# Gate and up products as three float32r products of split operands, and a ring of three query and key buffers

## The reference

```python
h = _layernorm(x) * (1 + ca) + sa
Q, K, V = ...                                  # 16 heads of 16
scores = Q @ K.T / 4 + slopes * (k - q)        # causal, then softmax
x = x + ga * ((softmax(scores) @ V) @ o_w.T + o_b)
h = _layernorm(x) * (1 + cb) + sb
hq = fp4_quant_dequant(h)                      # blocks of 16: grid value times the block's scale
gate = hq @ fp4_quant_dequant(w_gate).T        # w_gate, w_up: 704 x 256
y = hq @ fp4_quant_dequant(w_up).T
z = fp4_quant_dequant(silu(gate) * y)
x = x + gb * (z @ fp4_quant_dequant(w_down).T) # w_down: 256 x 704
```

## Time and profile before

| | |
|---|---|
| median of 3 runs | 3683.75 us (3681.61 to 3691.07) |
| the profiled execution, its own time | 3689.2 us |
| its span, first to last instruction | 3687.4 us |
| mean granted TensorE clock | 0.979 of full speed |
| PE, DVE, ACT, POOL busy | 94%, 81%, 52%, 35% of the span |

### The profile page before, as it was taken

The page is one execution under the profiler, slowest core; times in us unless marked ns, Lnnn a source line. Parts: engine busy times, 40 slices in busy tenths (PEclk is TensorE's granted clock), DMA queues, the critical chain, the costliest instruction groups (busy, mean ns, idle before and its releaser), DMA issues.

```text
span 3687.4 us, 56900 instructions
## 1 busy us (share of the span) xinstructions
PE 3475.3 (94%) x20920; PEld 1926.6 (52%) x20920; DVE 2993.7 (81%) x5836; ACT 1924.8 (52%) x3631; POOL 1272.5 (35%) x919
## 2 busy tenths in 40 slices
PE   6889999999999999999999999999999999999987
PEld 2335555555555555555555555555555555555555
DVE  9987978788787888878788787888878788786855
ACT  3455555555555555555555555555555555554541
POOL 5213424243342423324243332523324243342233
PEclk7899999999999999999999999999999999999998
DMA  7242423314333332423314333342423314333010
GB/s 128 41 88 43 70 50 59 66 32 74 53 56 59 50 67 43 70 50 59 66 32 74 53 58 57 50 71 38 71 50 62 64 34 71 53 52 52 23 28 12
DMA packets 160938, 205.34 MB, mean 56 GB/s; under 512 B 44740, under 2 KB 100628, under 8 KB 160660
## 3 DMA queue, kind: packets, MB, share of 16 engines
q1 hardware_dynamic: 160660, 201.69, 32.4%
HBM read 63.65 MB, written 17.89 MB: 22 GB/s over the span
## 4 chain that ended last, share of the span: by engine, by line
PE 69%; DVE 17%; ACT 5%; SPq 4%; DMA 3%; issue 2%; POOL 1%; ACTq 0%; POOLq 0%; DVEq 0%
PE banks L758 13%; PE banks L782 11%; PE banks L739 9%; PE banks L879 8%; PE banks L886 8%; PE banks L902 6%; PE banks L809 5%; DVE banks L1208 4%; DVE top L1206 4%; ACT arena L971 3%; PE banks L860 3%; SPq L619 2%; DMA sums<-oT 2%; PE banks L742 1%; PE banks L895 1%
## 5 line engine op out<-in xcount | busy, mean ns | idle before, releaser
L971 ACT ACTIVATE arena<-banks 128x512 f32<-128x512 f32 (+1 forms) x2432 | 1235.0, 585 | 941.9 <-PE banks L758 508.5
L1208 DVE CUSTOM_DVE_ANT_0 banks<-banks,mask 128x640 f32<-128x640 f32 (+3 forms) x1024 | 1031.7, 1045 | 155.4 <-PE banks L782 147.5
L739 PE MATMUL banks<-qa,ka 105*128 105x512 bf16 (+3 forms) x3072 | 784.5, 329 | 52.4 <-ACT arena L971 27.2
L782 PE MATMUL banks<-ka,qa 102*128 102x512 bf16 (+3 forms) x3072 | 751.5, 333 | 55.7 <-DVE top L1208 21.9
L758 PE MATMUL banks<-arena,va 128*17 128x512 f32 (+3 forms) x6144 | 585.6, 500 | 12.1 <-ACT arena L971 4.1
L1105 POOL TENSOR_TENSOR hid<-hid,tm 128x704 f32<-128x704 f32 x128 | 214.9, 1679 | 911.6 <-DVE hid L1182 911.6
L782 PEld LDWEIGHTS banks<-ka,qa 102*128 102x128 bf16 x3072 | 259.1, 99 | 421.9 <-DVE top L1208 103.5
L739 PEld LDWEIGHTS banks<-qa,ka 105*128 105x128 bf16 x3072 | 273.3, 97 | 392.5 <-ACT arena L971 126.9
L1206 DVE TENSOR_REDUCE top<-banks 128x2 f32<-128x768 f32 (+3 forms) x384 | 386.4, 1041 | 102.7 <-PE banks L787 101.2
L902 PE MATMUL banks<-wdT,hqT 128*128 128x256 f32 x1536 | 367.3, 390 | 4.1 <-ACT hqT L1014 3.8
L879 PE MATMUL banks<-wguT,xqT 128*128 128x352 f32 x1024 | 332.4, 467 | 3.2 <-ACT arena L971 2.5
(11 more groups left out here) (152 smaller groups left out, 4603.4 us busy)
## 6 DMA issues: line engine op xcount, KB each, us to landing
qa<-parts SPq DMA_DIRECT2D x384, 128.0 KB, 4.6
ka<-parts SPq DMA_DIRECT2D x384, 128.0 KB, 6.3
xa<-in_x SPq DMA_DIRECT2D x16, 1024.0 KB, 10.1
xr<-in_x SPq DMA_DIRECT2D x64, 256.0 KB, 2.7
out_x<-xr SPq DMA_DIRECT2D x64, 256.0 KB, 3.4
rsumT<-rsum_dram SPq DMA_DIRECT2D x63, 256.0 KB
onT<-oT SPq DMA_DIRECT2D x252, 64.0 KB, 4.1
ffn_rows<-rows_dram SPq DMA_DIRECT2D x16, 256.0 KB, 3.2
```

The lines of the kernel that those rows point to most:

```text
L739: mm = pe.matmul(ps[:, m * w:(m + 1) * w], ka[g][0:KT, h, kt * P:(kt + 1) * P], qa[g][0:KT, h, q0:q0 + w], start=heads < G and m == 0, sto ...
L782: mm = pe.matmul(ps[:, at:at + z - a], qa[g][0:KS, h0 + m, qt * P:(qt + 1) * P], ka[g][0:KS, h0 + m, a:z], start=qt > 0 and m % paired == ...
L971: nc.scalar.activation(probs[:, s % P_SLOTS, j * heads:(j + 1) * heads, 0:w], ps[:, 0:heads * w].rearrange("p (h q) -> p h q", h=heads), A ...
L1208: nc.vector.tensor_tensor_reduce(out=ps, in0=ps, in1=mask[:, S - w:S], scale=1.0, scalar=MASKED, op0=ALU.add, op1=ALU.max, accum_out=tops) ...
```

## The change

- **Products.** `xqT` and `wguT` each become two float32r tensors, high and low. The high part is ScalarE's copy of the PSUM bank into a float32r tensor; the low part is a new DVE instruction (XL for the rows, WL for the weights) that subtracts the high part from the same bank. A product is high x high, high x low, low x high, summed in PSUM: three float32r matmuls in place of one float32 matmul. GA waits for XL through `low_done`, and the bank of XT and of WT is held until DVE has read it.
- **Ring.** There are three buffers of queries and keys in place of four, used in turn: group n (counted over all batches) has buffer n mod 3, and its MOVE waits for the last T of group n - 3, in place of n - 4. In the plan it also stands behind TOP of group n - 2, and its due time is later by a quarter of a batch.
- **Slope rows.** A buffer no longer belongs to one group, so the six slope rows have to be renewed each time. QROW writes them into borrowed memory (`slope_stage`), SROW copies them to DRAM (two DMAs per group, once), and each MOVE of queries begins with a seventh DMA that brings them in. KROW fills three buffers.
- **Plan.** `SHIFT` has other numbers, the planned costs of GA and UP are 0.95 and 1.9 in place of 1.2 and 2.4, and the U events have later due times.

The diff, its added and removed lines only, cut to the core:

```diff
+LANDED = {"q": 16 * (len(Q_PARTS) + 1), "k": 16 * len(K_PARTS)}
+SETS = 3
+def earlier(b, g, n):
+    return divmod(b * NG + g - n, NG)
...
-    SHIFT = {"ACT CO": 42.0, "ACT GA": -43.0, "ACT HT": -8.0, "ACT KROW": 78.0, "ACT LX": 22.0, "ACT T": -74.0,
...
+    SHIFT = {"ACT CO": 32.0, "ACT GA": -46.0, "ACT HT": -5.0, "ACT KROW": 62.0, "ACT LX": 2.0, "ACT T": -104.0,
...
-            p.add("SP", ("MOVE", b, u, g), 3.9, at + (g + 1) * L / NG, ("POOL", ("SPL", b, u)),
-                  ("PE", ("T", b - 1, g, NS - 1, jobs_of(NS - 1) - 1)), ("SP", ("TOP", b - 1, g + 1)) if g + 1 < NG else None, lag=6.0)
+            p.add("SP", ("MOVE", b, u, g), 4.5 if UNITS[u][0] == "q" else 3.9, at + (g + 2) * L / NG, ("POOL", ("SPL", b, u)),
+                  ("PE", ("T", *earlier(b, g, SETS), NS - 1, jobs_of(NS - 1) - 1)), ("SP", ("TOP", *earlier(b, g, SETS - 1))),
+                  ("SP", ("SROW", 0, g)) if b == 0 else None, lag=6.0)
...
-            p.add("DVE", ("QROW", 0, g), 2.8, -30.0 + 20.0 * g, ("DVE", ("QROW", 0, g - 1)))
-            p.add("ACT", ("KROW", 0, g), 3.6, -30.0 + 20.0 * g, ("ACT", ("KROW", 0, g - 1)))
+            p.add("DVE", ("QROW", 0, g), 4.8, -60.0 + 5.0 * g, ("DVE", ("QROW", 0, g - 1)), ("SP", ("SROW", 0, g - 1)))
+            p.add("SP", ("SROW", 0, g), 1.3, -60.0 + 5.0 * g, ("DVE", ("QROW", 0, g)), lag=4.0)
+            if g < SETS:
...
-               ring="A", on="ACT", takes_cost=0.59)
+               ring="A", on="ACT", takes_cost=0.59, holder=("DVE", ("XL", b, r)))
+            p.add("DVE", ("XL", b, r), 0.69, due + 9, ("ACT", ("XT", b, r)))
-                    pe(("GA", b, t, k), 1.2, due + 10 + k, ("ACT", ("XT", b, r)), ("PE", ("HT", *tile(2 * r - 1), 1)),
+                    pe(("GA", b, t, k), 0.95, due + 10 + k, ("DVE", ("XL", b, r)), ("DVE", ("WL", 0, GU // 2)), ("PE", ("HT", *tile(2 * r - 1), 1)),
-                pe(("UP", b, t), 2.4, late + 2, ("PE", ("GA", b, t, 1)), ("PE", ("UP", *tile(t - 1))), ring="D", on="DVE",
+                pe(("UP", b, t), 1.9, late + 2, ("PE", ("GA", b, t, 1)), ("PE", ("UP", *tile(t - 1))), ring="D", on="DVE",
...
+LOW = {e: n for n, e in enumerate((e for e in PLAN.order["DVE"] if e[0] in ("WL", "XL")), 1)}
+WEIGHTS_LOW = max(LOW["WL", 0, n] for n in range(GU // 2 + 1))
...
-        qa = [sb(f"qa{g}", [P, G, S], BF16) for g in range(NG)]
-        ka = [sb(f"ka{g}", [P, G, S], BF16) for g in range(NG)]
+        qa = [sb(f"qa{n}", [P, G, S], BF16) for n in range(SETS)]
+        ka = [sb(f"ka{n}", [P, G, S], BF16) for n in range(SETS)]
-        xqT = [sb(f"xqT{n}", [P, C, 2 * P]) for n in range(2)]
+        xqT = [[sb(f"xqT{part}{n}", [P, C, 2 * P], F32R) for part in "hl"] for n in range(2)]
-        wguT = sb("wguT", [P, C, 2 * FF])
+        wguT = [sb(f"wguT{part}", [P, C, 2 * FF], F32R) for part in "hl"]
...
+        slope_stage = [t.bitcast(BF16) for t in (rsumT[:, :], onT[:, C - 1, :])]
...
-                    dst, order = (qa[g], Q_PARTS) if name == "q" else (ka[g], K_PARTS)
+                    qs, ks = group_set(b, g)
+                    dst, order = (qs, Q_PARTS) if name == "q" else (ks, K_PARTS)
-                    if b:
-                        sp.wait_ge(a_full, in_a["T", b - 1, g, NS - 1, jobs_of(NS - 1) - 1])
+                    if b * NG + g >= SETS:
+                        sp.wait_ge(a_full, in_a["T", *earlier(b, g, SETS), NS - 1, jobs_of(NS - 1) - 1])
+                    if name == "q":
+                        if b == 0:
+                            sp.wait_ge(slopes_out, 32 * g + 32)
+                        sp.dma_start(dst[SPLIT:KS, :, :].rearrange("p h q -> p (h q)"), slope_dram[g]).then_inc(part_in[u, g], 16)
-                    sp.dma_start(qa[g][KS:KT, :, :], topT[g % 2][:, :]).then_inc(top_in[g], 16)
+                    sp.dma_start(group_set(b, g)[0][KS:KT, :, :], topT[g % 2][:, :]).then_inc(top_in[g], 16)
+                elif kind == "SROW":
+                    g = e[2]
+                    sp.wait_ge(static_rows, G * g + G)
+                    for n in range(2):
+                        sp.dma_start(slope_dram[g][:, 2 * n * S:(2 * n + 2) * S], slope_stage[n][SPLIT:KS, :]).then_inc(slopes_out, 16)
...
+                low = [LOW[o] for o in PLAN.before[e] if o in LOW]
+                if low:
+                    pe.wait_ge(low_done, max(low))
...
-                        src = xqT[(t // 2) % 2][:, :, (t % 2) * P:(t % 2 + 1) * P]
+                        high, low = (part[:, :, (t % 2) * P:(t % 2 + 1) * P] for part in xqT[(t // 2) % 2])
+                        terms = [(x[:, c, :], w[:, c, :]) for c in range(C) for x, w in ((high, wguT[0]), (high, wguT[1]), (low, wguT[0]))]
-                            for c in range(C):
-                                mm = pe.matmul(ps[:, 0:FH], src[:, c, :], wguT[:, c, e[3] * FH:(e[3] + 1) * FH],
-                                               start=(c == 0), stop=(c == C - 1))
+                            pe.wait_ge(low_done, max(LOW["XL", b, t // 2], WEIGHTS_LOW))
+                            for n, (x, w) in enumerate(terms):
+                                mm = pe.matmul(ps[:, 0:FH], x, w[:, e[3] * FH:(e[3] + 1) * FH],
+                                               start=(n == 0), stop=(n == len(terms) - 1))
-                                for c in range(C):
-                                    mm = pe.matmul(ps[:, k * BANK:k * BANK + FH], src[:, c, :],
-                                                   wguT[:, c, FF + k * FH:FF + (k + 1) * FH],
-                                                   start=(c == 0), stop=(c == C - 1))
+                                for n, (x, w) in enumerate(terms):
+                                    mm = pe.matmul(ps[:, k * BANK:k * BANK + FH], x, w[:, FF + k * FH:FF + (k + 1) * FH],
+                                                   start=(n == 0), stop=(n == len(terms) - 1))
...
-                        nc.scalar.copy(xqT[e[2] % 2][:, :, :], ps[:, :].rearrange("p (c n) -> p c n", c=C)).then_inc(a_free, 1)
+                        nc.scalar.copy(xqT[e[2] % 2][0][:, :, :], ps[:, :].rearrange("p (c n) -> p c n", c=C)).then_inc(a_free, 1)
...
+                        if g:
+                            dve.wait_ge(slopes_out, 32 * g)
-                            nc.vector.tensor_scalar(qa[g][SPLIT:KS, i, :], ones[SPLIT:KS, :],
+                            nc.vector.tensor_scalar(slope_stage[i // 2][SPLIT:KS, i % 2 * S:(i % 2 + 1) * S], ones[SPLIT:KS, :],
...
+                        r = e[2]
+                        high, low = xqT[r % 2]
+                        dve.wait_ge(a_free, in_a["XT", b, r])
+                        nc.vector.tensor_tensor(low[:, :, :], bank(("XT", b, r)).rearrange("p (c n) -> p c n", c=C),
+                                                high[:, :, :].bitcast(F32), ALU.subtract).then_inc(low_done, 1)
```

More of the change, by code:

```diff
@@ L12 @@
 BF16 = mybir.dt.bfloat16
+F32R = mybir.dt.float32r
 I32 = mybir.dt.int32
@@ L229, in plan, with pe @@
     L = 240.0
-    def pe(event, cost, due, *after, ring, on, takes_cost, then=(), lock=None, banks=1):
-        p.add("PE", event, cost, due, *after, lag=0.22, ring=ring, lock=lock, banks=banks)
+    def pe(event, cost, due, *after, ring, on, takes_cost, then=(), lock=None, banks=1, holder=None):
+        p.add("PE", event, cost, due, *after, lag=0.22, ring=ring, lock=lock, banks=banks, holder=holder)
         p.add(on, event, takes_cost, due, ("PE", event), *then, takes=ring)
@@ L277, in maxima @@
                    *([("SP", ("MOVE", b, u, g)) for u in (2 * (g // 2), 2 * (g // 2) + 1)]
-                     + [("DVE", ("QROW", b, g)), ("ACT", ("KROW", b, g))] if j == 0 else ()),
+                     + [("ACT", ("KROW", b, g))] if j == 0 else ()),
                    ring="D", on="DVE", takes_cost=(0.14 if w <= BANK else 0.29) + 1.042e-3 * w * heads, banks=-(-heads * tile_pitch(heads, w) // BANK),
@@ L326, in normalise @@
         p.add("SP", ("RDW", b, g, *half), 0.7, due, ("DVE", ("RD", b, g, *half)), ("SP", ("RBC", *old)), lag=6.0)
-        p.add("SP", ("RBC", b, g, *half), 0.7, due, ("SP", ("RDW", b, g, *half)), ("POOL", ("MUL", b, g // 2 - 1) if g >= 2 else ("MUL", b - 1, C - 1)), lag=7.0)
+        p.add("SP", ("RBC", b, g, *half), 0.7, due, ("SP", ("RDW", b, g, *half)), ("SP", ("SROW", 0, NG - 1)), ("POOL", ("MUL", b, g // 2 - 1) if g >= 2 else ("MUL", b - 1, C - 1)), lag=7.0)
         if g % 2:
@@ L542, in bank, with group_set @@
             return banks[:, first * BANK:(first + number) * BANK]
+        def group_set(b, g):
+            n = (b * NG + g) % SETS
+            return qa[n], ka[n]
         in_a, in_d, in_q = NUMBER["A"], NUMBER["D"], NUMBER["Q"]
@@ L990, in run @@
                         act.wait_ge(a_full, full)
-                        nc.scalar.copy(wguT[:, :, 2 * n * P:(2 * n + tiles) * P],
+                        nc.scalar.copy(wguT[0][:, :, 2 * n * P:(2 * n + tiles) * P],
```

(2 more changed lines are left out.)

49 lines of the change are left out of this document (33 added, 16 removed), and 13 rows, old and new, of the table SHIFT.

## The result

The changed kernel takes 3574.58 us in the median (3573.87 to 3578.04) against 3682.95 us (3681.61 to 3691.07) for the kernel before, measured side by side. The ratio is 0.9703, with a 95% interval of 0.9686 to 0.972. The forecast was 3574.

What follows compares the result with a forecast made beforehand. PE was taken as the bound, with DVE near enough to disturb it. Fifteen batches at 7.5 us won give 112.5; with 7 lost at the start and 4 won at the end, 109.5 us, so 3574 median, range 3530 to 3640.

Steps and rivals of the forecast that it cites:

- start: Before batch 1: QROW's waiting rounds and WL's six subtractions, less a quantising pass moved back, lose 7 us, 0 to 15.
- PE's busy time in a batch: Gate and up products: 3.60 us a tile in place of 4.73, so 9.0 us less for a batch of eight tiles.
- last batch and its end: Batch 15's feed-forward runs alone: 6 us won on its chain pieces, 2 us given back to XL, 4 us won taken.
- I take the lower bound, 0.150: Gate and up products: a float32r matmul of 352 columns streams one column per clock, as bfloat16, and costs 0.150 us.
- neither bound: Price of a 352-column float32r matmul: between 0.150 us at one clock per column and 0.296 us at two.
- rival of two clocks per column: Gate and up products: float32r streams at 0.296 us a matmul, 7.10 us a tile, total about 3985 us; chance 6%.
- My estimate by that rule: Gate and up products with every weight load added: a tile goes from 6.4 to 6.1 us, little won.
- rival of the loads as the pace: Gate and up products: weight loads of 0.190 us set the pace, 4.56 us a tile, total 3680 us; chance 4%.
- I take the middle, 1.5 us: PE's idle time per batch: grows 1.5 us, between none and 3.0, as DVE's free time falls from 39.7 to 29.
- the rival took 4.8: GA waits for DVE's late XL, about 1.2 us for each of four pairs, 4.8 a batch, total 3646 us; chance 17%.
- 40 us of slack on SP: Ring and slope DMA: MOVE needs 15 us of a group's 55, so both were priced at nothing.
- moves too late: SP reaches MOVE over 40 us late, S starts late, each microsecond per group costs 64; 3766 us at 3 us; chance 2%.

Runs made afterwards that it cites:

- one-product kernel: Changed kernel, order and XLs kept, but gate and up each one float32 product of the unsplit operand: 3687.66 us, ratio 0.9999 to the kernel before.
- bfloat16 run: Changed kernel with the high and low tensors in bfloat16 in place of float32r, same 24 matmuls a tile: 3546.36 us in one run.
- old table: Changed kernel with only SHIFT put back to the numbers of the kernel before, new U due times kept: 3719.12 us, ratio 1.0091 to the kernel before.
- ring alone: Changed kernel with single float32 products, no XL or WL: 3689.40 us with new SHIFT and U due times, 3755.69 us with those of the kernel before.
- Table b: Changed kernel with another SHIFT, found by small random steps that did not lengthen the planned time: 3561.11 us, ratio 0.9661 to the kernel before.

## Why the prediction came out right, step by step

Its mechanism holds: cheaper products shorten PE's busy time, PE stays the bound, and ring, slope rows and XL are hidden, XL all but half a microsecond a batch. The range is earned by that. That the total was hit to 1 us is luck, since the start came out 14.5 us better than entered and the end 14.5 us worse. The terms:

| term | predicted | measured |
|---|---|---|
| one float32r matmul, 352 columns | 0.150 us | 0.159 us |
| PE's busy time in a batch | -9.0 us | -7.8 us |
| PE's idle time in a batch | +1.5 us | -0.1 us |
| a batch | 7.5 us won | 7.85 us won |
| start | 7 us lost | 7.5 us won |
| last batch and its end | 7.5 + 4 us won | 3.0 us lost |

**The products.** The step "I take the lower bound, 0.150" was 9 ns short. 24 x 0.159 is 3.82 us a tile, 0.91 less than before and not 1.13, 7.3 us a batch; the one-product kernel, its order held fixed, has 7.1 us more of PE's busy time a batch and a period 7.0 longer. The rest of the 7.8 us came with the order and the clock. The bfloat16 run shows that the working was right for that type and that float32r carries 10 ns more. The spacing crossed neither bound and stayed under 0.16. The weight loads, 188 ns each, don't set the pace: matmuls stand 0.159 and 0.13 us apart. A float32r matmul takes one pass of its columns, and the rival of two clocks per column is out. The Trainium skill's "TensorE: Matmul & The Clock Gate" ("The mechanism") says that a load overlaps matmuls in flight only when it goes to another row group; these rows contradict that, as the earlier trace rows do. The same section of the Trainium skill also lets a load into the array's spare weight buffer go ahead, which these rows would fit. My estimate by that rule had a slip, 24 x 0.257 is 6.2 us and not 6.1. So had the rival of the loads as the pace: it comes to some 3689 us and not 3680 (20 won, 22.5 lost to idle time, 3 at the two ends).

**PE's idle time.** The step "I take the middle, 1.5 us" entered a cost that is not there. Idle time stayed at 7.9 us, though DVE's free time fell by 14 us where I had worked out 11: DVE is busy 186.5 us a batch, 6.0 more than before, and XL is only 2.7 of them. That free time is no measure: with DVE busy 188.7 PE is idle 13.7 us under the old table, with 186.5 it is 7.9 under the new one, and the ring alone with its two tables has 10.9 and 8.0. The order of the lists matters more. The error of the spacing (192 x 9 ns, 1.7 us a batch) and this one (1.6) cancelled, which is luck too.

**XL.** Its 0.69 us (686 ns in the median) and the cover for GA's wait are confirmed: 1.5 us of waiting in all, and without XL thirteen of the periods are 0.5 us shorter, where the rival took 4.8.

**Ring and slope rows at nothing.** Right for the kernel as it is: 0.9994 to 1.0012 for the ring alone, nothing from the slope DMAs. But the reason given, 40 us of slack on SP, was too weak. With that slack and the old table the ring costs 68 us. The rival "moves too late" priced this as S standing for MOVE. No run shows PE stand there for long; the loss comes with the order that the planner builds under the ring's rules.

**Start.** QROW's four rounds ran as described, and their waits for the copies were short. Timeline of DVE:

```profile
37.62 3.47 DVE L1291 TENSOR_SCALAR rsumT<-arena,xb 6x1024 bf16<-6x1024 f32 x2 [4.60 <-DMA slope_dram<-onT]
...
47.62 2.56 DVE L1291 TENSOR_SCALAR rsumT<-arena,xb 6x1024 bf16<-6x1024 f32 x2 [2.10 <-DMA slope_dram<-onT]
...
71.71 5.80 DVE L1251 TENSOR_REDUCE top<-banks 128x4 f32<-128x512 f32 x6
```

6.70 us of waiting, and the first eviction of S at 71.71, 3.2 us earlier than before, not later. The products give 4.2 us up to batch 1 (one product against after), the order 3.3.

**End.** The products pay there as worked out, 12.4 us against 11.5. But the order lost 15 where I had entered nothing. In the chain of after, a gate product early in the feed-forward of batch 15 and the next one are 29.8 us apart:

```profile
3467.49 3.86 PE banks L925 x12
3471.35 2.60 PE banks L932 x12
...
3497.28 3.18 PE banks L925 x12
```

The corresponding pieces of before, 3585.88 and 3609.18, are 23.3 us apart. In the one-product kernel they are 30.4 us apart, so the gap belongs to the order. DVE spends 6 us of it on residual additions and statistics of other rows (3483.30 to 3489.15). The clock adds to it: in the product behind the gap it was 0.58, which took 3.18 us for what takes 1.93 at 3521.23, where before has 1.00 in this place. (In the first of the two it was low in both kernels, 0.50 and 0.53.) Gap and clock make up about half of the 15 us; the rest was not located. Table b has an end of 313.4 us. Which entry of the table does it was not tried.

**What stays open.** Which of the new rules makes the old table so bad (the moves' due times, their wait for TOP) was not separated; the ring alone loses 68 us without the new U due times. The three products in the old order with four buffers were not tried either. Why float32r costs 10 ns more per matmul than bfloat16 is not known.

## What to carry to other kernels

A float32 product on a PE-bound stretch can be had as three float32r matmuls of split operands for 0.81 of the time (3.82 against 4.73 us a tile), if the subtraction for the low part fits beside other work and the memory for the second copies is there. It leaves out low x low. Where a program lays out its order from a table, a change of its dependencies and the table go together: the same edit was worth -3.0% with one and +0.9% with the other, so it should not be judged under the old one. Read busy and idle time of the bound engine over whole periods, with the granted clock beside them, and not the free time of its neighbour; and cut the run into start, periods and end before believing a total that fits.
